# P turned by 64-row transposes in one run a unit, in a fused RWKV and local-attention kernel on one core

## What is computed

```python
q, k = rotary_xpos(l2norm(q) * qs, l2norm(k) * ksc)
bk, bv = look_around(bk), look_around(bv)          # previous window and this one: 256 keys
sim = jnp.einsum('bhwid,bhwjd->bhwij', bq, bk)
sim = jnp.where(mask, -jnp.finfo(sim.dtype).max, sim)
attn = jax.nn.softmax(sim, axis=-1)
out = jnp.einsum('bhwij,bhwjd->bhwid', attn, bv)
x = x + o @ wo
h = layernorm(shift_token(x)) @ w1 + b1            # 256 -> 2 x 682
x = x + (a * gelu(g)) @ w2 + b2
```

## Time and profile before

| | us |
|---|---|
| median of 3 runs (2856.03 to 2857.04) | 2856.45 |
| the profiled execution's own time | 2855.33 |
| its span in the profile | 2853.2 |
| PE busy | 2750.0 (96%) |
| PEld (weight loads) busy | 2496.1 (87%) |
| DVE busy | 2325.1 (81%) |
| ACT busy | 2284.3 (80%) |
| POOL busy | 1637.9 (57%) |
| granted TensorE clock, mean | 0.988 |

### The profile page before, as it was taken

One profiled execution on the slowest core, in us unless ns is written; L12 is line 12 of the kernel. 1 busy time (PEld: TensorE's weight loads), 2 busy tenths in 40 slices (PEclk: granted clock), 3 DMA queues, 4 the chain that ended last, 5 costly groups with the idle time before them and its releaser, 6 DMA issues.

```text
span 2853.2 us, 75604 instructions
## 1 busy us (share of the span) xinstructions
PE 2750.0 (96%) x27108; PEld 2496.1 (87%) x27108; DVE 2325.1 (81%) x6459; ACT 2284.3 (80%) x5557; POOL 1637.9 (57%) x1652
## 2 busy tenths in 40 slices
PE   7999948999999999999999999999999999999998
PEld 6888836899999999999999899899999999999998
DVE  3979978988888888888888787888888888888884
ACT  4979956788888888888888788888888888888885
POOL 2323317666666666666666565666666666666653
PEclk9999979999999999999999999999999999999999
DMA  3252111121121112111111213111111111111111
GB/s 101 65 186 72 40 59 58 51 57 57 48 55 53 48 55 57 57 50 53 53 50 50 85 57 102 50 50 50 46 50 47 49 46 48 50 50 50 50 39 46
DMA packets 211334, 166.75 MB, mean 58 GB/s; under 512 B 21522, under 2 KB 206612, under 8 KB 209940
## 3 DMA queue, kind: packets, MB, share of 16 engines
q1 hardware_dynamic: 139284, 127.82, 14.8%
q10 hardware_dynamic: 71680, 34.10, 4.2%
HBM read 110.89 MB, written 42.58 MB: 54 GB/s over the span
## 4 chain that ended last, share of the span: by engine, by line
PE 84%; DVE 8%; issue 3%; ACT 2%; DMA 2%; SPq 1%; POOL 1%; ACTq 0%; DVEq 0%; POOLq 0%
PE ps L397 31%; PE ps L396 17%; PE ps L363 10%; PE ps L472 7%; PE ps L460 6%; PE ps L488 4%; DVE Sm L1112 3%; PE ps L445 3%; PE ps L498 2%; DVE Ar L1083 1%; DVE oTl L1135 1%; PE ps L524 1%; PE ps L423 1%; DMA oF<-ro_scratch 1%; PE ps L350 1%
## 5 line engine op out<-in xcount | busy, mean ns | idle before, releaser
L761 ACT ACTIVATE Sm<-Sm,nb 128x256 f32<-128x256 f32 (+1 forms) x1024 | 503.1, 496 | 1.4 <-DVE nb L1112 0.7
L1112 DVE CUSTOM_DVE_ANT_0 Sm<-ps,mask,sc 128x256 f32<-128x256 f32 (+1 forms) x1024 | 420.3, 475 | 77.3 <-PE ps L460 37.7
L1257 POOL TENSOR_TENSOR rs<-rs,mhalf 128x8 f32<-128x8 f32 x256 | 422.1, 1649 | 14.2
L1345 POOL TENSOR_TENSOR uTl<-Gl,uTh 128x512 fp32r<-128x512 f32 (+1 forms) x192 | 212.1, 1105 | 327.8 <-ACT uTh L834 219.7
L396 PE MATMUL ps<-zTh,W1h 128*128 128x256 f32 (+1 forms) x1408 | 375.6, 288 | 0.1
L741 ACT ACTIVATE sq<-ps 128x512 f32<-128x512 f32 x256 | 151.5, 592 | 269.4 <-PE ps L397 265.7
L396 PE MATMUL ps<-zTh,W1l 128*128 128x256 f32 (+1 forms) x1408 | 365.7, 282 | 0.0
L1184 DVE SCALAR_TENSOR_TENSOR Gl<-ps,vecs,Gl 128x256 f32<-128x256 f32 (+1 forms) x384 | 172.0, 476 | 219.8 <-PE ps L396 118.8
L397 PE MATMUL ps<-WQh,hTh 128*128 128x512 f32 x768 | 339.3, 442 | 2.8 <-ACT hTh L735 2.8
L397 PE MATMUL ps<-WQl,hTh 128*128 128x512 f32 x768 | 302.9, 394 | 0.0
L1356 POOL TENSOR_TENSOR Ar<-Ar,Br 128x512 f32<-128x512 f32 x128 | 164.6, 1286 | 219.9 <-DVE Br L1085 219.9
(11 more groups left out here) (190 smaller groups left out, 8645.7 us busy)
## 6 DMA issues: line engine op xcount, KB each, us to landing
oF<-ro_scratch ACTq DMA_DIRECT2D x256, 128.0 KB, 3.1
tb<-tab SPq DMA_DIRECT2D x128, 128.0 KB, 2.3
xc<-x SPq DMA_DIRECT2D x32, 256.0 KB, 3.0
rwkv_scratch<-rw SPq DMA_DIRECT2D x32, 256.0 KB, 2.7
rk<-rwkv_scratch SPq DMA_DIRECT2D x64, 128.0 KB, 2.3
xin<-x SPq DMA_DIRECT2D x64, 128.0 KB, 2.3
x_scratch<-x SPq DMA_DIRECT2D x64, 128.0 KB, 1.7
y_scratch<-os SPq DMA_DIRECT2D x64, 128.0 KB, 4.2
```

The costliest lines, as they stand in the source:

```text
L761: act.activation(Sm[:, h, c0:c1_], Sm[:, h, c0:c1_], ACT.Exp, bias=nb[:, h:h + 1], scale=-1.0, accum_out=sm[:, n % 2, h:h + 1]).then_inc(S ...
L1112: dve.tensor_tensor_reduce(Sm[:, h, c0:c1_], PS[:, bank["scores", n, q, h % 2], (h // 2 % 2) * 256 + c0:(h // 2 % 2) * 256 + c1_], mask[:, ...
L1257: return pool.tensor_tensor(ap, ap, mhalf[:, 0:ap.shape[-1]], ALU.pow)
L1345: pool.tensor_tensor(uT[1][:, j, :], Gl[:, g, :], uT[0][:, j, :].bitcast(F32), ALU.subtract).then_inc(S["ul"], 1)
```

## The change

The 16 transposes of 128 x 128 a unit become 32 of 64 queries by 128 keys: the stationary operand is 64 rows (queries) of Sm by 128 keys, the moving one the 64 x 64 corner of ident on the same rows, so that each writes 128 partitions by 64 columns. Transposes on rows 0-63 and 64-127 alternate and write two different banks. `turn_p` is called twice (four heads each) instead of four times, and the two calls stand together: in odd steps right before the scores, behind both w2_mm, and in even steps between mlp parts 1 and 2. The order of banks and the lists of ScalarE, VectorE and Pool follow. `p_out` still copies 4 x 512 columns, now each bank's four heads by two sides by 64 queries into pieces of 64 columns. Each copy waits for its whole call.

```diff
             def turn_p(n, j):
-                c0, c1_ = cols(n)
-                k = bank["turn", n, j]
-                w.wait_ge(S["ex"], 8 * n + 2 * j + 2)
-                w.wait_ge(*read_out(former["turn", n, j]))
-                for i in range(2):
-                    for c in range(c0, c1_, 128):
-                        ins = pe.transpose(PS[:, k, i * 256 + c:i * 256 + c + 128], Sm[:, 2 * j + i, c:c + 128],
-                                           ident[:, :])
+
+                sides = [n % 2] if first_win(n) else [0, 1]
+                w.wait_ge(S["ex"], 8 * n + 4 * j + 4)
+                for r in range(2):
+                    w.wait_ge(*read_out(former["turn", n, j, r]))
+                for h in range(4):
+                    for s in sides:
+                        for r in range(2):
+                            rows = slice(64 * r, 64 * r + 64)
+                            at = h * 128 + s * 64
+                            ins = pe.transpose(PS[:, bank["turn", n, j, r], at:at + 64],
+                                               Sm[rows, 4 * j + h, s * 128:(s + 1) * 128], ident[rows, rows])
                 ins.then_inc(S["p5"], 1)
...
-            def p_out(n, j):
-                c0, c1_ = cols(n)
-                w.wait_ge(S["p5"], 4 * n + j + 1)
-                w.wait_ge(S["p6"], 2 * (n - 1) + j // 2 + 1)
-                act.activation(PT[:, 2 * j:2 * j + 2, c0:c1_],
-                               PS[:, bank["turn", n, j], :].rearrange("p (h j) -> p h j", h=2)[:, :, c0:c1_],
+            def p_out(n, j, r):
+                sides = slice(n % 2, n % 2 + 1) if first_win(n) else slice(0, 2)
+                w.wait_ge(S["p5"], 2 * n + j + 1)
+                w.wait_ge(S["p6"], 2 * (n - 1) + j + 1)
+                act.activation(PT[:, 4 * j:4 * j + 4, :].rearrange("p h (s t) -> p h s t", s=2)[
+                                   :, :, sides, 64 * r:64 * r + 64],
+                               PS[:, bank["turn", n, j, r], :].rearrange("p (h s t) -> p h s t", h=4, s=2)[:, :, sides, :],
                                ACT.Copy).then_inc(S["pt"], 1)
...
-                    w.wait_ge(S["p5"], 4 * (n - 1) + h // 2 + 1)
+                    w.wait_ge(S["p5"], 2 * (n - 1) + q + 1)
...
+                    if live(11):
+                        mlp((t - 11) // 2, 0)
+                        mlp((t - 11) // 2, 1)
+                    if live(5):
+                        turn_p(t - 5, 0)
+                        turn_p(t - 5, 1)
+                    if live(11):
+                        mlp((t - 11) // 2, 2)
...
+                    if live(13):
+                        w2_mm(t - 13)
+                    if live(12):
+                        w2_mm(t - 12)
+                    if live(5):
+                        turn_p(t - 5, 0)
+                        turn_p(t - 5, 1)
+                    if live(4):
+                        scores(t - 4, 0)
+                        scores(t - 4, 1)
```

More of the change, by code:

```diff
@@ L98, in live @@
         return 0 <= t - d < U
[L100 to L134, removed]
@@ L312, in read_out @@
             if what == "turn":
-                return S["pt"], 4 * n + i[0] + 1
+                return S["pt"], 4 * n + 2 * i[0] + i[1] + 1
             if what == "scores":
@@ L569, in live @@
                     return 0 <= t - d < U
[L571 to L589, removed]
-                if live(5):
-                    turn_p(t - 5, 2)
-                    turn_p(t - 5, 3)
-                if live(11) and odd:
-                    mlp((t - 11) // 2, 2)
-                if live(4):
-                    scores(t - 4, 0)
-                    scores(t - 4, 1)
-                if live(2):
-                    qkv(t - 2, 1)
@@ L839, in live @@
                     return 0 <= t - d < U
-                odd = 1 - t % 2
-                if live(6):
-                    o_out(t - 6)
-                if live(5):
-                    exp(t - 5, 1)
-                if live(10) and not odd:
-                    z_out(t - 10)
-                if live(11) and odd:
-                    gelu((t - 11) // 2, 0)
-                if live(5):
-                    p_out(t - 5, 0)
-                    p_out(t - 5, 1)
-                if live(11) and odd:
-                    u_hi((t - 11) // 2, 0)
-                    gelu((t - 11) // 2, 1)
@@ L856, in scalar_program @@
-                if live(5):
-                    p_out(t - 5, 2)
-                    p_out(t - 5, 3)
-                if live(11) and odd:
-                    u_hi((t - 11) // 2, 1)
-                    gelu((t - 11) // 2, 2)
-                if live(6):
-                    oT_hi(t - 6)
-                if live(2):
-                    square(t - 2, 1)
-                if live(11) and odd:
-                    u_hi((t - 11) // 2, 2)
-                if live(0) and t < NG:
-                    pre_norm(t)
@@ L1217, in vector_program @@
-                if live(12) and not odd:
-                    x3_out(t - 13)
-                if live(11) and odd:
-                    glu((t - 11) // 2, 1)
-                if live(12) and not odd:
-                    x3_out(t - 12)
-                if live(11) and odd:
-                    glu((t - 11) // 2, 2)
-                if live(4):
-                    masked_max(t - 4, 0)
-                    masked_max(t - 4, 1)
-                if live(1) and t - 1 < NG:
-                    pre_y(t - 1)
```

425 lines of the change are left out of this document (320 added, 105 removed).

## The result

The changed kernel takes **2851.56 us** (median of 18 runs, 2849.89 to 2854.07), the kernel before on the same chips 2856.43 (18 runs, 2855.02 to 2858.42). The ratio is 0.9983, 95% interval 0.9976 to 0.9990: 4.9 us less, 0.17%, where 37 were forecast. The profiled execution took 2851.76 us, with a span of 2849.7 (before 2853.2).

The account below looks back on a forecast made before the run. TensorE was taken to bound the kernel, until VectorE or ScalarE is late; 26 layer 0 pairs x 0.26 and 31 layer 1 pairs x 0.96 gave -36.6 us, so 2819 us, range 2790 to 2856.

Parts of the forecast that it names:

- Pace of the turn: Turning P: 16 pairs of short transposes 0.058 us apart, a run of 0.93 us, bounds 0.055 and 0.11 a pair.
- Rivals 1 and 4: Turn: 1, pairs load-bound at 0.11 us, 2884 us; 4, short transposes can't issue that fast; together chance 0.16.
- Changes of the array: TensorE between full array and row halves: 0.21 us in, 0.19 out; even steps pay 0.40, odd steps nothing added.
- Layer 0, even step: Four P copies ahead of u_hi 1 delay gelu 2, glu 2 and pre_mm: step 0.55 us longer.
- the chain that was named: Layer 0, even step: gelu 1, four copies, u_hi 1, gelu 2, glu 2, then pre_mm, 0.55 us later.
- Odd steps: TensorE's own sum, 0.93 - 1.74 = -0.81 us a step, passes in full in both layers.
- Scores and qkv 1 take banks that the four copies free: Waits added: behind these banks only TensorE would wait; copies end about a microsecond before qkv 1 starts.
- exps close to late: Odd steps: the turn's second half waits for all eight exps; cost 0, bounds 0 and 0.1 us a pair.
- Layer 1, even step: VectorE and PV can hardly move ahead: -0.15 us taken of the possible -0.41.
- Steps outside the pairs: The first six steps and the last few: 0, bounds 0 and -7 us together.
- rival 3: ScalarE eats the gain: slower copies or late glu 2, 0.4 us an even step; 2842 to no change; chance 0.22.

Follow-up runs that it names:

- the z copies alone: The change, but in odd steps ScalarE does both units' z copies (zTh) behind both z rows, VectorE's order untouched; 2841.3 us, 0.9948 of the kernel before.
- e3_full_array: The change's order of work on all engines, but with the 16 full 128x128 transposes of before; 2880.6 us, 1.0082 of the kernel before.

## Why the prediction was wrong

- **Pace of the turn: right, a little low.** 0.058 us a pair was taken, 0.062 is measured (3 ns, then 58 to 61), with 0.11 once after the first pair: 0.99 us from first to last start for 0.93. Rivals 1 and 4 are out. The Trainium skill's figure for a weight load (TensorE: Matmul & The Clock Gate, section LDWEIGHTS (loading the stationary operand)), by which the run would have been an estimated 1.7 us, does not hold for these transposes: the trace shows 0.99.
- **Changes of the array: right, with some luck.** In the even step TensorE's own list is 0.41 shorter, as summed, but two small errors cancel: the run is 0.06 longer than taken, and going in and out costs about 0.35 instead of 0.40 (starts 0.21 apart before the run and 0.15 and 0.22 behind it, less two spacings of 0.12). Between turn and scores the assumption was zero; where nothing is late it is 0.03 from start to start.
- **Layer 0, even step: right.** +0.55 forecast, +0.61 measured (26 x 0.06 = 1.6 us), by the chain that was named; moving two copies took it away.
- **Odd steps: this step failed.** "TensorE's own sum: odd step -0.81" was passed on whole, with only VectorE's masked_max looked at as a possible successor (idle 1.45 in the earlier trace rows). The sentence "Scores and qkv 1 take banks that the four copies free" is wrong for odd steps: the scores take the banks of wo, zT and the two w2 products, and the readers of the first two had only 0.4 to 0.45 us of room. Of the 0.81, 0.06 was the run's size; the rest of what was missing, 0.38 in layer 0 and 0.41 in layer 1, were waits, since taking them away gave 16.33 and 15.56. Over the pairs that is 26 x 0.38 + 31 x 0.41 = 22.6 us of the 33.1 by which the span missed the forecast. The run's size adds 57 x 0.06 = 3.4. For layer 1 the z copies alone show it with nothing given back in the even step. For layer 0 no run does: with the odd step at 16.33 the even one took 0.20 more, so that 0.18 a pair is shown. The "exps close to late" were costed at 0, bounds to 0.1: they cost 0.13 in layer 1.
- **Layer 1, even step: better than forecast** (-0.30 for -0.15), 31 x 0.15 = 4.7 us the other way.
- **Single steps of layer 1.** Added up, its pairs gained 15.4 us and not 31 x 0.64 = 19.8. The largest exception is t = 76, 1.5 us longer than before. There, and at the change of layers (t = 66, 1.0 longer), TensorE waits before the turn for VectorE's x2_out: 1.41 and 6.12 us, before 0.22 and 4.24. With the old transposes in the new order (e3_full_array) it waits 0.55 and 5.76, so part of it comes with the order; the rest stays open.
- **Steps outside the pairs: forecast 0, bounds 0 and -7; measured +5.5, so the sign was wrong.** The first PV starts 1.4 us later (464.4 for 463.0; over all kernels here it lies between 462.1 and 464.8, whatever their transposes). The first six steps take 92.7 instead of 88.5. Only t = 6 and t = 9 are longer, by 2.5 and 2.7, and in each of these TensorE's clock was at 1.2 GHz for 6.8 us, where before it was in none of the six. But with the old transposes in the new order, and 3.4 us at 1.2 GHz, they take 91.1, so the cause stays open.
- The range held the time only by its top end, which stood for rival 3; the chance of 0.77 was for a gain of over 0.2%, and the measured one is 0.17%. Rival 3 named the right outcome, a gain eaten by waits up to no change, and the exps; but it looked to ScalarE in even steps, and gave it a third of 0.22.

## What to carry to other kernels

Before a gain on the bounding engine is passed on, list for its next stage every buffer that it takes and who empties it, and read how long before each was ready: the smallest of these distances, less what the hand-over itself takes (here 0.10 to 0.145 us), and not the idle time of one engine, is how much can be gained there. An order of work can cost more than a shape brings; take the two apart, as here with the old transposes in the new order. Where several readers are due at once, exchanging them moved the wait here; what helped was to put behind them work that nobody waits for, and even that cost something where the moved work ran beside another engine's.

## What the runs showed of the hardware

A run of short transposes needs no gap before products on the same row halves (0.03 us from start to start, then 0.20 to the second pair, together no more than two spacings of 0.12), while between products on the full array it starts 0.21 after the one ahead, and the two products behind it come after 0.15 and 0.22, where 0.12 is the pace. The Trainium skill (TensorEngine Tiling (Array Packing), section Tiling Modes) says that a change of mode, and not of the tile alone, drains the engine. The trace agrees as far as the price goes: it is paid between the full array and row halves, and not between transposes and products that both work on 64 x 128.

TensorE's clock was granted less in the first steps of the kernels with the shorter turn. Busy times and granted clock from 425 to 600 us, of before and of the change:

```profile
425.00:600.00 175.00, 156.85 (x1575) 133.88 (x1574) 150.27 (x452) 130.47 (x367) 120.45 (x122) 0.96 0.19 55
```

```profile
425.00:600.00 175.00, 148.98 (x1670) 128.31 (x1669) 147.16 (x441) 126.39 (x359) 116.14 (x117) 0.93 0.18 52
```

The three kernels with full transposes throughout had 10 to 14 us at 1.2 GHz in this stretch, the change 24, the others with short ones throughout 24 to 34, and the one with eight units of full ones 20. One of the change's drops comes at 516.2 us, inside the second of two waits of TensorE (timeline of PE); the score pairs behind it are 0.21 apart where those ahead are 0.12:

```profile
514.29 0.71 PE L507 MATMUL ps<-ident,Sm 64*128 64x64 f32 x16 [1.37 <-ACT Sm L820]
...
515.38 0.28 PE L491 MATMUL ps<-kTh,qTl 64*128 64x256 f32 x2
515.49 0.28 PE L491 MATMUL ps<-kTl,qTh 64*128 64x256 f32 x2
517.19 0.58 PE L491 MATMUL ps<-kTh,qTh 64*128 64x256 f32 x2 [1.41 <-DVE x L1237]
517.54 0.45 PE L491 MATMUL ps<-kTh,qTl 64*128 64x256 f32 x2
517.75 0.45 PE L491 MATMUL ps<-kTl,qTh 64*128 64x256 f32 x2
```

That the shorter turn is the cause was tried for the first eight units and not settled.
